# A second buffer for the decay steps, an earlier order in group 0, and identity products behind attention, in a one-core perceiver layer

## The reference

```
x = x + xattn(layernorm(x), ctx)   # 32 heads of 128, 4 key/value heads, 2176 keys
x = x + mamba(layernorm(x))        # 128 heads of 64, 8 groups, state 128, one chunk of 128 rows
x = x + ffn(layernorm(x))          # 56 blocks of 32: in each, only the largest of a rank-16 score is kept
```

```
dt    = softplus(dt + dt_bias);  a = -exp(A_log) * dt
L     = exp(segment_sum(a))                 # lower triangle, 128 x 128 for each head
y     = ((C_g B_g^T) * L) @ (xc * dt) + D * xc
out  += (y * norm_w * silu(gate)) @ out_proj    # and a root mean square over all of y
```

## Time and profile before

| | |
|---|---|
| median of 3 runs | 699.45 us (698.38 to 700.05) |
| profiled execution | 698.99 us, its span 697.3 us |
| TensorE busy | 671.9 us (96%), 4450 products |
| DVE / ACT / POOL busy | 436.9 / 356.7 / 117.1 us |
| mean granted TensorE clock | 0.988 |

### The profile page before, as it was taken

The page is one execution under the profiler, slowest core; times in us unless marked ns, Lnnn a source line. Parts: engine busy times, 40 slices in busy tenths (PEclk is TensorE's granted clock), DMA queues, the critical chain, the costliest instruction groups (busy, mean ns, idle before and its releaser), DMA issues.

```text
span 697.3 us, 12695 instructions
## 1 busy us (share of the span) xinstructions
PE 671.9 (96%) x4450; PEld 575.4 (83%) x4450; DVE 436.9 (63%) x1095; ACT 356.7 (51%) x706; POOL 117.1 (17%) x75
## 2 busy tenths in 40 slices
PE   7999998999999999999999987997999999999897
PEld 6888887899999999999999977996797797796453
DVE  2533115767777777677677765779857757756562
ACT  4403116667776677678766652664435435434101
POOL 0000001112431143114321133022220220200100
PEclk9999999999999999999999999998999999999989
DMA  8511001011021110311031503953577667647702
GB/s 257 240 61 60 1 1 61 1 56 67 1 71 52 64 56 0 120 60 60 0 111 50 240 12 145 293 199 144 203 242 264 223 238 274 214 175 276 283 20 98
DMA packets 15701, 87.07 MB, mean 125 GB/s; under 512 B 3584, under 2 KB 3968, under 8 KB 6064
## 3 DMA queue, kind: packets, MB, share of 16 engines
q1 hardware_dynamic: 15088, 85.52, 34.0%
q10 hardware_dynamic: 576, 1.05, 0.5%
HBM read 86.30 MB, written 0.26 MB: 124 GB/s over the span
## 4 chain that ended last, share of the span: by engine, by line
PE 92%; DVE 4%; ACT 2%; DMA 1%; issue 1%; SPq 0%; DVEq 0%; ACTq 0%
PE ps L1284 18%; PE ps L1079 15%; PE ps L1080 15%; PE ps L1081 14%; PE ps L1191 8%; PE ps L1324 8%; PE ps L1148 4%; PE ps L1313 2%; PE ps L1396 2%; PE ps L1431 2%; DMA ring<-wk_dram 1%; PE ps L1295 1%; PE ps L1304 1%; PE ps L1296 1%; DVE acc L922 1%; ACT prob L524 1%
## 5 line engine op out<-in xcount | busy, mean ns | idle before, releaser
L711 DVE TENSOR_TENSOR pt_lo<-ps,pt_hi 128x512 fp32r<-128x512 f32 x144 | 95.1, 661 | 72.0 <-ACT pt_hi L442 71.1
L1284 PEld LDWEIGHTS ps<-norm_t,ring 128*128 128x128 f32 x1152 | 132.6, 193 | 4.8 <-issue 3.9
L1284 PE MATMUL ps<-norm_t,ring 128*128 128x128 f32 x1152 | 133.8, 276 | 0.0
L442 ACT ACTIVATE pt_hi<-ps 128x512 fp32r<-128x512 f32 x144 | 82.2, 571 | 85.0 <-PE ps L1191 84.7
L524 ACT ACTIVATE prob<-prob,neg_max 128x512 f32<-128x512 f32 (+1 forms) x128 | 94.6, 741 | 7.5 <-DVE neg_max L803 7.5
L922 DVE SCALAR_TENSOR_TENSOR acc<-raw,cw,acc 128x127 f32<-128x127 f32 (+2 forms) x240 | 78.5, 402 | 27.9 <-ACT acc L622 27.9
L799 DVE TENSOR_SCALAR_CACHE_REDUCE prob<-ps 128x512 f32<-128x512 f32 (+1 forms) x160 | 92.0, 605 | 2.6 <-PE ps L1081 1.2
L1079 PE MATMUL ps<-pt_hi,v_hi 128*128 128x256 f32 x272 | 88.3, 325 | 0.0
L1191 PE MATMUL ps<-ident,prob 128*128 128x128 f32 x544 | 83.2, 273 | 1.9 <-DVE pt_lo L711 1.3
L1191 PEld LDWEIGHTS ps<-ident,prob 128*128 128x128 f32 x544 | 65.2, 140 | 14.9 <-DVE pt_lo L711 2.2
L1080 PE MATMUL ps<-pt_hi,v_lo 128*128 128x256 f32 x272 | 76.4, 281 | 0.0
(11 more groups left out here) (170 smaller groups left out, 1097.6 us busy)
## 6 DMA issues: line engine op xcount, KB each, us to landing
ring<-w_in_dram SPq DMA_DIRECT2D x36, 1024.0 KB, 4.8
ring<-w_out_dram SPq DMA_DIRECT2D x16, 1024.0 KB, 4.8
ring<-wq_dram SPq DMA_DIRECT2D x8, 1024.0 KB, 5.9
ring<-wo_dram SPq DMA_DIRECT2D x8, 1024.0 KB, 4.8
ring<-w_dram SPq DMA_DIRECT2D x4, 896.0 KB, 6.0
ring<-ctx_t_dram SPq DMA_DIRECT2D x3, 1024.0 KB, 6.8
ring<-w_dram SPq DMA_DIRECT2D x3, 1024.0 KB, 4.7
ring<-wk_dram SPq DMA_DIRECT2D x4, 256.0 KB, 8.2
```

The source lines that it names most:

```text
L442: copy = lambda dst, src: nc.scalar.activation(dst, src, ACT.Copy)
L711: sub = lambda dst, a, hi: nc.vector.tensor_tensor(dst, a, hi, ALU.subtract)
L1284: ins = mm(ps[:, bank, t * T:t * T + T], w[:, t, c, :], norm_t[:, c, :], start=(c == 0), stop=(c == NC - 1))
```

## The change

- `at_hi` and `at_lo` become two buffers each, and group `g` uses number `g % 2`. The new ones lie behind all others of the stage.
- POOL no longer waits for `seg_ps` 2 before `steps_a(1)`. The waits of the later groups stay as they are.
- TensorE: `segments(1, 1, 1)` stands ahead of `y_product(0, 0)` and no longer behind it.
- DVE: `skip_add(0, 0)` stands ahead of both masks of group 1 and no longer between them; `x_times_dt(1)` moves ahead of `gate(0, 0)` and `add_squares(0)`; groups 1 and 2 are written out, and the loop has two turns.
- TensorE: twelve products of the identity with itself, into bank 5, between the last `output` of attention and `norm_transpose(1, 7)`.

```diff
-                at_hi = sbuf(st4, "at_hi", [P, HPG, T], F32R)
-                at_lo = sbuf(st4, "at_lo", [P, HPG, T], F32R)
+                at_hi = [sbuf(st4, "at_hi0", [P, HPG, T], F32R)]
+                at_lo = [sbuf(st4, "at_lo0", [P, HPG, T], F32R)]
...
+                at_hi.append(sbuf(st4, "at_hi1", [P, HPG, T], F32R))
+                at_lo.append(sbuf(st4, "at_lo1", [P, HPG, T], F32R))
...
-                for dst, src in ((at_hi, a_hi), (at_lo, a_lo)):
+                for dst, src in ((at_hi[g % 2], a_hi), (at_lo[g % 2], a_lo)):
...
             steps_a(0)
-            pool.wait_ge(seg_ps, 2)
             steps_a(1)
             for g in range(GROUPS - 2):
                 pool.wait_ge(seg_ps, 2 * g + 4)
...
             taps_of(9, 7, 1, 12)
+            skip_add(0, 0)
             mask_decay(1, 1, 0)
-            skip_add(0, 0)
             mask_decay(1, 1, 1)
+            x_times_dt(1)
             gate(0, 0)
             add_squares(0)
...
-                x_times_dt(g)
+                if not (isinstance(g, int) and g == 1):
+                    x_times_dt(g)
...
-            with dve.Fori(0, 3) as turn:
+            mamba_step(1, 1)
+            mamba_step(2, 0)
+            with dve.Fori(0, 2) as turn:
                 for i in range(2):
-                    mamba_step(turn * 2 + (i + 1), 1 - i)
+                    mamba_step(turn * 2 + (i + 3), 1 - i)
...
+            for _ in range(WARM):
+                mm(ps[:, 5, 0:P], ident[:], ident[:], start=True, stop=True)
             norm_transpose(1, 7)
...
             segments(1, 1, 0)
+            segments(1, 1, 1)
             y_product(0, 0)
-            segments(1, 1, 1)
             project(0, 3)
```

More of the change, by code:

```diff
@@ L1294, in segments @@
                     h = 8 * half + 4 * i
-                    mm(ps[:, 2 + i, :], upper_r[:], at_hi[:, h:h + 4, :].rearrange("p h t -> p (h t)"), start=True, stop=False)
-                    ins = mm(ps[:, 2 + i, :], upper_r[:], at_lo[:, h:h + 4, :].rearrange("p h t -> p (h t)"), start=False, stop=True)
+                    mm(ps[:, 2 + i, :], upper_r[:], at_hi[b][:, h:h + 4, :].rearrange("p h t -> p (h t)"), start=True, stop=False)
+                    ins = mm(ps[:, 2 + i, :], upper_r[:], at_lo[b][:, h:h + 4, :].rearrange("p h t -> p (h t)"), start=False, stop=True)
                 ins.then_inc(seg_ps, 1)
```

## The result

Six runs of the changed kernel gave a median of 695.16 us (694.04 to 695.90), six of the kernel before 698.50. The ratio is 0.9944, with a 95% interval of 0.9931 to 0.9958: faster by 3.9 us at the 699.45 of the prediction, where 5.9 were forecast. (0.9944 is also the ratio of the two means, 695.00 and 698.88; the medians lie 3.3 us apart.) The profiled execution took 695.40 us, its span 693.6; the one of before took 698.99. The forecast was right in its direction and its range; its time was 1.7 us too low, its gain 2.0 us too large.

A forecast was written before the change was run, and what follows sets the result against it. TensorE was taken as the bound, so only its idle or lower-clock time could pay. Gains of 1.7 us behind attention and 4.2 in group 0 took 699.45 to 693.5 us; range 690.8 to 696.9.

The forecast's parts named there:

- Part 1: Behind attention: twelve identity products fit TensorE's wait for `normed` and keep its clock full, gaining 1.7 us.
- a rival at 0.08: Behind attention: identity products give nothing (695.2 us), or run late at the lower clock (697.4 us); chance 0.08.
- Part 2: Group 0: earlier POOL steps and reordered TensorE and DVE work start group 1's x transposes 4.2 us sooner.
- POOL's hold-up moved from chunk 6 to chunk 7: Group 0, DVE: chunk 6's taps drop to 3.2 us, chunk 7's rise to about 6.6 us beside POOL.
- The sum: Whole kernel: 1.7 + 4.2 = 5.9 us gained, from 699.45 to 693.5 us.
- the rival with the clock: Group 0: TensorE's clock falls behind the new 2.6 us gap, costing 1.7 to 3.4 us; 695.2 to 696.9, chance 0.15.
- Two of the signs: State-space stage: forecast wrong if the clock falls again before 485 us, or an x transposes period is not 26 us.
- the 692.3 to 694.7 that had the chance of 0.58: Whole kernel: the prediction's own forecast interval in us, chance 0.58.
- Steps moved past something: Chunk 0's taps, meeting `steps_a(1)`, may end up to 3.4 us late; 4.9 us of DVE waits absorb it by `gm`.
- the slower rival: Later groups: POOL's hold-up recurs, each group 1 to 1.5 us longer; 699.5 to 702.5 us, chance 0.04.

The follow-up runs named there:

- Halves: Changed kernel with GpSimd's steps for group 2 split in two, released after the taps of chunks 5 and 7; 690.92 us, ratio 0.9869.
- segments behind: Changed kernel with `segments(1, 1, 1)` put back behind `y_product(0, 0)`; 691.45 us, ratio 0.9884.
- the second gap filled: Changed kernel plus twelve identity products in group 0's remaining gap, ahead of group 1's x transposes; 693.50 us, ratio 0.9913.
- the fastest kernel: Changed kernel, GpSimd's group 2 steps split in two, six identity products before attention's last output, twelve before `norm_transpose(2, 7)`; 687.92 us, ratio 0.9824.

## Why the prediction was right in its parts and short in its sum

- **Part 1.** Right: 1.62 us for 1.7. The block took 2.84 us for 2.7 and lay in the gap. Its condition, a clock that is full when the block starts, holds only in some executions, three of the seven profiles: 1.0 to 1.3 us are left where it does not (40.76 to 41.11 against 42.10). The prediction had this as a rival at 0.08, with the transposes 2.1 us late and nothing gained; they were 0.3 to 0.7 late. It had the whole block at the lower clock, 5.4 us, and the block took 3.8 to 4.2, since the clock was back before its end.
- **Part 2.** Right step by step: -4.18 for -4.2. Taps 3.21 for 3.2 and 6.70 for 6.6; TensorE waits of 1.11 and 2.63 us for 1.1 and 2.6. That POOL's hold-up moved from chunk 6 to chunk 7 was the term that mattered: it leaves the idle time behind which the clock fell. "Halves" shows what it is worth: 2.8 us of x(1), and the gap.
- **The sum.** This is where the prediction failed. It left the clock out behind the 2.6 us of idle time that its own steps gave. It had the rows for it, a fall behind 3.24 and behind 4.17 us of idle time, and took the held clock behind 1.8 us as the nearer one. The runs show falls behind 2.63 us and behind 1.82. Price: 1.7 of 3.4 us at 0.50, as the rival had it; 1.59 us measured by filling the gap, 1.30 against before. Two of the signs that the prediction named for being wrong came true: the clock fell before 485, at 480.9, and one period between x transposes was 27.60 us.
- **The place in the range.** 695.16 lies above the 692.3 to 694.7 that had the chance of 0.58, and at the lower end of the rival with the clock (695.2 to 696.9, chance 0.15). The range held because it took that rival in. That the forecast was 1.7 us too low, and the rival's price is 1.7 as well, is chance: beside the clock, the 0.85 us ahead of `normed` were missing too, and the median of before came out 0.95 us below the 699.45 of the forecast once three more runs were taken, which hides part of the 5.9 against 3.9.
- **Steps moved past something.** The taps of chunk 0 took 5.24 us beside `steps_a(1)`, and `gm` still waited 3.12 us for TensorE (3.19 before): nothing was left of it, as said. Every later group kept its 26.0 us, so the slower rival did not come about.
- **The remaining 0.85 us** lie ahead of `normed`, where the diff changes nothing. `normed` started between 420.72 and 422.25 in the twelve profiles. What sets that was not tried. In the profile after, the clock was 0.50 for 3.4 us at 9.9 us, in the one of before it was not. The seven profiles with such a stretch near the start have 421.43 to 422.25, the five without it 420.72 to 421.34. So every one with it is later, by 0.7 us in the mean; but either set spreads by 0.6 to 0.8 us, so the clock is not all of it. The diff is not known to have caused it.

## What to carry to other kernels

When a step is moved forward, look for whom it releases: here four products that came 2.5 us earlier (8.5 us behind gm, and 11.0 with the segments behind) started GpSimd in the middle of VectorE's critical taps. Put GpSimd's work beside VectorE operations that read one of their two inputs from PSUM, or into VectorE's waits, and split it if it does not fit. And price the idle time that a forecast leaves on TensorE, not only that which it removes: gaps of 2.6 and 3.1 us cost another 1.6 and 2.4 us here through the clock, and products that fill them cost nothing here as long as they ended before the wait did (x(1) at 17.98 us behind gm with the second gap filled, 17.99 without).

## What was not expected of the hardware

- An operation of VectorE with two SBUF inputs that meets an affine select of GpSimd waits until this is over: 0.34 us became 1.97 to 2.09, next to instructions of 2.0. Of the twelve taps beside a pair of GpSimd's instructions (chunk 6 before, chunk 7 after) two were held in this way, one by each instruction of the pair. With one input from PSUM it lost nothing (2.16 us for eight, with and without). Both agree with what the prediction took from the Trainium skill (GPSIMD Engine Reference, Key points: contention with VectorE instructions that have two SBUF inputs). The row of chunk 6's taps in the kernel before, in ns (shortest, median, longest):

```profile
L922 DVE SCALAR_TENSOR_TENSOR acc<-raw,cw,acc x12: 336/339/2084, 466.0 to 472.3; 128x127 f32<-128x127 f32 x4, 128x126 f32<-128x126 f32 x4, 128x125 f32<-128x125 f32 x4
```

- The clock can fall after TensorE has already resumed work: at 480.9, 0.8 us behind the gap's end, and at 418.1 in the middle of the output products behind a gap of 1.8 us. In other executions of nearly the same program it did not fall there. A single profile therefore doesn't show whether a gap is safe; behind a gap that was filled no fall was seen in any profile, but three of the five executions of the fastest kernel, whose profiles are not on record, had mean clocks of 0.997 and 0.998, so 3 to 4 us at 0.50 somewhere (an estimate: 0.002 to 0.003 of 686 us, doubled).
